# A cross-attention and mixture-of-experts layer on one core: another order of work at its beginning and in its last pair of batches

## The reference

```python
x = x + attention(layernorm(x), ctx)   # 16 heads of 16 channels, rotary positions on q and k,
                                       # query s sees keys s-64 .. s; projections q, k, v, o with biases
x2 = x
z = layernorm(x2)
top-2 of 8 experts by z @ router.T, softmax weights of the two
for each expert e:                     # gate, up: 1024x256, down: 256x1024
    y = (silu(z @ gate.T) * (z @ up.T)) @ down.T
    out += chosen(e) * y * mean weight of e over its tokens
```

## Time and profile before

| | before |
|---|---|
| median of 3 runs | 486.79 us (485.64 to 487.36) |
| profiled execution, own time | 483.92 us |
| its span | 482.1 us |
| TensorE (PE) busy | 446.3 us, 93% |
| VectorE (DVE) busy | 301.0 us, 62% |
| ScalarE (ACT) busy | 272.6 us, 57% |
| GpSimd (POOL) busy | 142.0 us, 29% |
| mean granted TensorE clock | 0.982 |

### The profile page before, as it was taken

How to read it: one execution, slowest core, us unless ns; L and a number is a source line. 1 busy time by engine, 2 the same in 40 slices (tenths; PEclk the granted TensorE clock), 3 DMA queues, 4 the chain that set the end, 5 groups by cost and what they waited for, 6 DMA issues and landing times.

```text
span 482.1 us, 8983 instructions
## 1 busy us (share of the span) xinstructions
PE 446.3 (93%) x2787; PEld 367.9 (76%) x2787; DVE 301.0 (62%) x735; ACT 272.6 (57%) x863; POOL 142.0 (29%) x174
## 2 busy tenths in 40 slices
PE   3898999999999999889999999999999999999980
PEld 2655666757565655569899999999999999999980
DVE  2565769898979878775737647466465473763330
ACT  1286887878788888335445545455464554554230
POOL 5111013544446262673023050140410502205013
PEclk9999999999999999989999999999999999999995
DMA  8173421111202020229956545565465553213002
GB/s 229 41 210 111 175 78 33 39 41 33 67 6 67 8 63 26 84 76 384 300 151 155 180 78 170 166 125 164 111 164 154 89 170 94 27 40 41 0 5 34
DMA packets 24588, 50.48 MB, mean 105 GB/s; under 512 B 5410, under 2 KB 15302, under 8 KB 24394
## 3 DMA queue, kind: packets, MB, share of 16 engines
q10 hardware_dynamic: 7886, 26.44, 17.6%
q1 hardware_dynamic: 10508, 16.47, 11.3%
q0 software_dynamic: 6144, 6.97, 8.8%
HBM read 39.62 MB, written 13.20 MB: 110 GB/s over the span
## 4 chain that ended last, share of the span: by engine, by line
PE 69%; DVE 7%; ACT 7%; DMA 5%; issue 5%; POOL 3%; ACTq 1%; POOLq 0%; SPq 0%; DVEq 0%
PE b_o L703 9%; PE b_small L703 8%; PE b_s L690 7%; PE b_s L692 7%; PE b_s L691 7%; PE b_s L445 6%; ACT probs L831 4%; PE b_pv L468 3%; PE b_proj L523 3%; PE b_pt L454 3%; PE b_pt L690 2%; PE b_pt L692 2%; PE b_pt L691 2%; PE b_proj L499 2%; DMA xin<-slots 2%
## 5 line engine op out<-in xcount | busy, mean ns | idle before, releaser
L831 ACT ACTIVATE probs<-b_s,negmax 100x100 f32<-100x100 f32 x256 | 85.4, 359 | 24.1 <-DVE negmax L1108 16.7
L1320 POOL DMA_INDIRECT out<-y_sb,idnow x32 | 49.7, 1552 | 158.7 <-ACT y_sb L869 151.4
L857 ACT CAST h_hi<-h_sb 128x448 fp32r<-128x448 f32 x64 | 36.3, 567 | 88.1 <-DVE h_sb L1185 88.1
L690 PE MATMUL b_s<-x_hi,w_hi 128*128 128x448 f32 x192 | 71.5, 372 | 0.0
L692 PE MATMUL b_s<-x_hi,w_lo 128*128 128x448 f32 x192 | 70.4, 367 | 0.0
L691 PE MATMUL b_s<-x_lo,w_hi 128*128 128x448 f32 x192 | 70.0, 364 | 0.0
L1086 DVE TENSOR_TENSOR w_lo<-w_raw,w_hi 128x1024 fp32r<-128x1024 f32 x48 | 58.8, 1225 | 13.8 <-ACT w_hi L792 13.4
L1189 DVE TENSOR_TENSOR h_lo<-h_sb,h_hi 128x448 fp32r<-128x448 f32 x64 | 40.0, 625 | 40.5 <-ACT h_hi L857 39.9
L831 ACT ACTIVATION_READ_ACCUMULATOR probs<-b_s,negmax 100x1 f32 x256 | 56.5, 221 | 0.0
L445 PE MATMUL b_s<-kblk,qrot 128*100 128x400 f32 x128 | 53.7, 500 | 0.0
L792 ACT CAST w_hi<-w_raw 128x1024 fp32r<-128x1024 f32 x48 | 50.4, 1050 | 0.0
(11 more groups left out here) (153 smaller groups left out, 969.5 us busy)
## 6 DMA issues: line engine op xcount, KB each, us to landing
w_raw<-in_ffw ACTq DMA_DIRECT2D x48, 512.0 KB, 3.9
xin<-slots SPq DMA_DIRECT2D x10, 449.8 KB, 4.4
slots<-in_padrows SPq DMA_DIRECT2D x9, 449.8 KB, 4.1
kblk<-krot SPq DMA_DIRECT2D x128, 12.5 KB
out<-x_all SPq DMA_DIRECT2D x8, 200.0 KB
ctx_all<-in_ctxT SPq DMA_DIRECT2D x1, 1200.0 KB, 6.5
x_all<-in_x SPq DMA_DIRECT2D x1, 1200.0 KB
attw<-in_wT ACTq DMA_DIRECT2D x2, 256.0 KB, 3.9
```

The lines of the kernel that those rows point to most:

```text
L690: pe.matmul(o, wh[:, c, cols], x_hi[:, c, :], start=(c == 0), stop=False)
L831: m = nc.scalar.activation(probs[:, N % 3, h, :], b_s[N % 3][0:S, h * S:(h + 1) * S], ACT.Exp, bias=negmax[:, N % 4, h:h + 1], accum_out=p ...
L857: nc.scalar.copy(h_hi[:, f, :], h_sb[:, f % 2, :]).then_inc(s_hhi, 1)
L1320: G.indirect_dma_start(out, bass.IndirectOffsetOnAxis(idnow[:, n:n + 1], 0), y_sb[:, n, :], None, bounds_check=TOK + TILE - 1, oob_is_err= ...
```

## The change

At the beginning:
- TensorE starts with 16 matmuls on a zeroed tile `blank` (`idle(16)`), and has more of them between the first projections.
- ScalarE loads its table with an Exp on `blank` right after its three loads; it also makes `ident_bf` and `mask_bf`. The query weights get a semaphore of their own (`s_wq`). The other loads move to SyncE, behind a wait for the constants `cst`.
- VectorE writes xn, rotates, and makes the eight key blocks of half c = 0 of pair 0 itself (`first_key_blocks`), by a multiplication with a 0/1 column for each head (`C_HEAD`). SyncE makes the other eight.

In the last pair:
- The rows that are transposed for the logits are only centred (`rows_center`); 1/deviation comes in at the difference of the two best logits.
- The sums over `chosen` and over the weights are made by TensorE with more matmuls in place of additions on VectorE and GpSimd.
- ScalarE makes three of the four comparisons, as `relu(1 - |slot - here|)` in two passes (`near_columns`); VectorE the fourth (`hot_column`). GpSimd makes the low parts (`rows_low`), and issues all eight last scatters behind its weight sums.
- `hidden` starts with the products that need the high part alone, and `take_ids(0)` stands behind block `FC - 3`.

```diff
@@ SyncE
             sp.dma_start(cst[:, :], consts).then_inc(s_cst, 16)
+            sp.wait_ge(s_cst, 16)
+            sp.dma_start(attw[:, 2:4], wT[:, 2:4]).then_inc(s_w, 16)
+            sp.dma_start(biasrow[:, :, :], brow).then_inc(s_w, 16)
+            sp.dma_start(rw_sb[:, :, :], rwT).then_inc(s_w, 16)
+            sp.dma_start(rows_sb[:, :], rownum).then_inc(s_w, 16)
             load_rows(1, 1, 2)
...
-                for c in range(DC):
+                for c in range(0 if i else 1, DC):
@@ TensorE
+            def idle(count):
+                for _ in range(count):
+                    pe.matmul(b_s[0][:, 0:QH * S], blank[:, 0:P], blank[:, :], start=True, stop=True)
...
                         warm(3)
+                        x2_transpose(NPAIR - 1)
...
+                if i == NPAIR - 1:
+                    pe.matmul(o[:, E:2 * E], ones_bf[0:S, 0:S], chosen[:, 0, :], start=False, stop=False)
+                    pe.matmul(o, ones_bf[0:S, 0:S], before[:, 0:1, :].to_broadcast([S, 2, E]),
+                              start=False, stop=True).then_inc(s_rk, 1)
...
-            pe.wait_ge(s_ch, NPAIR)
-            small_free()
-            pe.matmul(b_small[:, 0:E], ones_bf[0:S, :], before[:, 2, :],
-                      start=True, stop=True).then_inc(s_cnt, 1)
+            pe.wait_ge(s_rkc, NPAIR - 1)
+            for k, counts in enumerate((before[:, 0, :], chosen[:, 0, :], chosen[:, 1, :])):
+                m = pe.matmul(b_pt[:, 0:E], ones_bf[0:S, :], counts, start=(k == 0), stop=(k == 2))
+            m.then_inc(s_cnt, 1)
             warm(4)
             late_rows(NPAIR - 1)
...
+            for k in range(TOPK * 2 + 1):
+                part = wsel[:, k - 1, :] if k else wacc[:, :]
+                m = pe.matmul(b_o[:, 0:E], cst[0:S, C_ONE:C_ONE + P], part,
+                              start=(k == 0), stop=(k == TOPK * 2))
@@ ScalarE
+            def near_columns(i, b):
+                last = i == NPAIR - 1
+                a.wait_ge(s_here, 2 if last else 1)
...
+                nc.scalar.activation(onehot[:, b, :], slot_sb[:, :], ACT.Abs, bias=here[:, b:b + 1], scale=-1.0
+                                     ).then_inc(s_abs, 1)
+                a.wait_ge(s_abs, done)
+                nc.scalar.activation(onehot[:, b, :], onehot[:, b, :], ACT.Relu, bias=1.0, scale=-1.0
+                                     ).then_inc(s_hotA, 1)
@@ VectorE
+            def first_key_blocks(half):
+                v.wait_ge(s_krot, 1)
+                v.wait_ge(s_zero, 3)
+                for h in range(half * QH, (half + 1) * QH):
+                    V.tensor_scalar(kblk[:, 0, 0, h, :], krot[:, 0:2, :].rearrange("p b s -> p (b s)"),
+                                    cst[:, C_HEAD + h:C_HEAD + h + 1], None, ALU.mult).then_inc(s_kblk[0], 16)
...
+            def rows_center(i):
+                v.wait_ge(s_var2, i + 1)
+                for b in range(2):
+                    ins = V.tensor_scalar(xn[:, b, :], x_all[:, 2 * i + b, :], mv2[:, b, 0:1], None, ALU.subtract)
+                ins.then_inc(s_xc, 1)
...
-                    if e == 0 and split and f == FC - 5:
+                    if e == 0 and split and f == FC - 3:
                         take_ids(0)
@@ GpSimd
+                if i == NPAIR - 1:
+                    rows_low(NPAIR - 2)
                 if i == NPAIR:
-                    scatter(i - 2, range(TOPK))
-            scatter(NPAIR - 2, range(TOPK, TOPK * 2))
+                    rows_low(NPAIR - 1)
+            scatter(NPAIR - 2)
             scatter(NPAIR - 1)
```

More of the change, by code:

```diff
@@ L597, in late_rows @@
                 for b in range(2):
-                    pe.wait_ge(s_hot, 2 * (i - NPAIR + 2) + b + 1)
+                    if last and b == 0:
+                        pe.wait_ge(s_hot, 1)
+                    else:
+                        pe.wait_ge(s_hotA, 3 if last else b + 1)
                     for c in range(DC):
@@ L627, in _ @@
                         den_transpose(2 * i - 1)
-                    if n == 0 and i == NPAIR + 1:
-                        warm(3)
-                    if n == 0 and 0 <= i - 2 < NPAIR:
+                    if n == 0 and 0 <= i - 2 < NPAIR - 1:
                         x2_transpose(i - 2)
                     if n == 0 and i == NPAIR + 1:
-                        warm(2)
+                        warm(1)
                     if n == 3 and nxt:
+                        if i < 0:
+                            idle(2)
                         q_project(i + 1)
+                        if i < 0:
+                            idle(3)
                     if 0 <= N - 2 < NQ * NPAIR:
@@ L646, in _ @@
                     if n == 1 and nxt:
+                        if i < 0:
+                            idle(8)
                         xn_transpose(i + 1)
@@ L688, in hidden @@
                         if f == 0 and which == 0:
+                            pe.wait_ge(s_xhi, DC * t + c + 1)
+                        pe.matmul(o, wl[:, c, cols], x_hi[:, c, :], start=(c == 0), stop=False)
+                        pe.matmul(o, wh[:, c, cols], x_hi[:, c, :], start=False, stop=False)
+                        if f == 0 and which == 0:
                             pe.wait_ge(s_xlo, DC * t + c + 1)
-                        pe.matmul(o, wh[:, c, cols], x_hi[:, c, :], start=(c == 0), stop=False)
-                        pe.matmul(o, wh[:, c, cols], x_lo[:, c, :], start=False, stop=False)
-                        m = pe.matmul(o, wl[:, c, cols], x_hi[:, c, :], start=False, stop=(c == DC - 1))
+                        m = pe.matmul(o, wh[:, c, cols], x_lo[:, c, :], start=False, stop=(c == DC - 1))
                     m.then_inc(done, 1)
@@ L741, in _ @@
             a.dma_start(attb[:, :, :], bT).then_inc(s_wk, 16)
[L742 to L746, removed]
+            a.dma_start(attw[:, 0], wT[:, 0]).then_inc(s_wq, 16)
+            a.wait_ge(s_blank, 1)
+            nc.scalar.activation(table[:, :], blank[0:1, 0:1], ACT.Exp)
             def evac_proj(i, which, ready, done):
@@ L840, in _ @@
                         evac_proj(i + 1, 1, s_k, s_kc)
+                    if n == 0 and i < 0:
+                        a.wait_ge(s_cst, 16)
+                        nc.scalar.copy(ident_bf[:, :], cst[:, C_ID:C_ID + P]).then_inc(s_setup, 1)
+                        nc.scalar.copy(mask_bf[:, :, :], cst[:, C_MASK:C_MASK + S].unsqueeze(1)
+                                       .to_broadcast([P, QH, S])).then_inc(s_setup, 1)
                     if n == 2 and nxt:
                         evac_proj(i + 1, 0, s_q, s_qc)
+            near_columns(NPAIR - 1, 1)
             def x_high(t):
@@ L1142, in _ @@
                         destinations(i - 2)
[L1143 removed]
+                    if n == 5 and nxt and i >= 0:
                         q_rotate(i + 1)
```

165 lines of the change are left out of this document (113 added, 52 removed).

## The result

The changed kernel takes 490.48 us (median of 13 runs, 489.46 to 492.37), the kernel before 486.95 (13 runs, 484.73 to 489.95): ratio 1.0081, 95% interval 1.0059 to 1.0102, 3.5 us slower. The profiled execution has a span of 488.1, 6.0 more than that of before.

A forecast was written before the change was run, and what follows sets the result against it. TensorE, 93% busy, was taken as the bound, with time lost only where it stands or runs at half clock. Beginning -3.5, tile 1 +2.3 and clock +2.8 sum to +1.6 us: 488.4 on the median, range 485.5 to 491.5.

The forecast's parts named there:

- The beginning: Start of the kernel: VectorE's value write at 17.2 instead of 20.74, -3.5 us, handed through by attention.
- The last scatter unchanged: GpSimd, last pair: last scatter issued at 220.6, the time of before, with the beginning's 3.5 left out.
- The tile's start: TensorE begins the first expert tile at 213.7 instead of 214.98, with the beginning's 3.5 left out.
- rival 3: Clock falls in the last pair as before, delaying VectorE's count: 2 us more on tile 1, 490.5; chance 0.12.
- The copy directly behind the sixth block: VectorE's copy of tile 0's ids at 236.5, after 20.2 us of its own work, without waiting for the ids.
- Tile 1: TensorE goes on with tile 1 at 242.6 instead of 240.32, after the later ids copy: +2.3 us.
- The clock behind the gap: TensorE stands 6.5 us before tile 1, then runs at low clock: +2.8 us, bounds 0 and 3.4.
- the transposes waiting 5 us or more: Sign in the profile after: tile 1's transposes wait 5 us or more for a transfer; wrong if under 2.
- The chances: Probabilities against the kernel before: faster 0.30, within about 0.3% (1.5 us) 0.26, slower 0.44.
- (2): Last pair pays: tile starts early enough, tile 1 lands at 240 or before, no long gap: 482.5; chance 0.24.
- (1): Gap before tile 1 costs no clock, or the transfer lands fast; halves cancel: 485.6; chance 0.18.
- (4): Constants land last anyway, xn no earlier: the beginning gives -1 instead of -3.5, 491; chance 0.04.

The follow-up runs named there:

- e7: Kernel before with only the idle matmuls of the new beginning (16, 8, 2 and 3) added: 486.64 us, ratio 0.9999.
- e2: Kernel before with the copy of tile 0's ids moved behind the sixth hidden block: 493.06 us, ratio 1.0114.
- e12: Same program as e4 (kernel before with the new beginning alone), run again on another chip: 480.85 us, ratio 0.9909.
- e4: Kernel before with the change's beginning alone, old last pair: 479.67 us, ratio 0.9854.
- e9: Changed kernel, ids copy still behind the sixth block, with ten more matmuls of no use in the last pair: 486.23 us, ratio 0.9993.
- e1: Changed kernel with the copy of tile 0's ids put back behind the fourth hidden block: 482.83 us, ratio 0.9917.
- e3: Changed kernel with 28 matmuls of no use on TensorE ahead of tile 1's transposes: 488.70 us.
- e5: Kernel before with the change's last pair alone, ids copy left behind the fourth block: 488.07 us, ratio 1.0021.
- e8: e1 with ScalarE's three comparisons put back on VectorE: 482.36 us.
- e6: e1 with ten more matmuls of no use on TensorE in the last pair: 481.59 us, ratio 0.9892.
- e10: e9 with the copy of tile 0's ids behind the fifth hidden block instead of the sixth: 483.01 us.
- e11: e10 with the low parts on VectorE and two of pair 6's scatters ahead of GpSimd's last weight sums: 482.47 us, ratio 0.9926.

## Why the forecast came out as it did

The direction and the mechanism of the loss were right: the moved line, the wait it makes and the low clock behind it. The number, 488.4 against 490.48, is close partly by luck. It was made of two terms that were both too small, the gain of the beginning and the cost on the way to tile 1, and their errors have opposite signs.

- **The beginning, forecast -3.5.** The value write was 2.8 earlier in the profile of after, the 12th maximum 3.4; the low stretch at 46 us took part of it back, so that 2.1 were left at the last maximum. The value write alone is no measure of the gain (e7: as early, and nothing gained). On the medians the beginning alone is worth 5.5 to 7.5. The step that failed is the sum's base: it was made against one execution that lay 2.9 below the median, and the difference was left unexplained. Part of it is half clock: both projections of the old beginning run at it, until 21 us in the kernel before and until 26 in e2; the new one has it for 3.4 us or not at all (e12, e4). The prediction read the clock from the page as full there, although its own sum sets the projection's 1.59, called warm, where 3.03 stood.
- **The last scatter unchanged, forecast 220.6 in the time of before.** It came at 219.26, with the 2.1 added back 221.4; from the last maximum 27.9 against 27.1 before. ScalarE's and VectorE's savings did not reach GpSimd. Right to within 1.
- **The tile's start, forecast 213.7.** Measured 215.61, or 217.7 with the 2.1 added back: 4.0 late. The forecast had the last pair at full clock; it ran at 0.51 from 207 to 217. That is rival 3's mechanism, which I gave 0.12 because "four busy stretches close up". They did not: TensorE was busy 5.28 of 7 us before the fall, and then each placing matmul and each of the ten sums took about double. Ten more matmuls of no use took 4.2 out (e9). About 0.8 of the 4.0 was lost before the fall: ScalarE ended its four passes for pair 6 at 206.62 (208.7 with the 2.1 added back), forecast 207.9.
- **The copy directly behind the sixth block.** VectorE's count from the first product to the copy, forecast 20.2, was 20.1. Only its start was late.
- **Tile 1, forecast +2.3.** Measured 4.3 in absolute time, 6.4 from the last maximum, that is with the beginning taken out. e1 and e2 show that the moved line does it: 4.7 less one way, 6.3 more the other.
- **The clock behind the gap, forecast +2.8.** Measured 1.7 (e3: 1.8 on the medians, 1.7 in the profile).

In the profiles: -2.1 + 6.4 + 1.7 = +6.0, the difference of the spans, where the forecast had +1.6. On the medians it is +3.5: the profiled execution of the kernel before lies 3.0 below its median, that of the changed kernel 0.6 below. Some 1.8 of this stand at the beginning (3.5 between the means of the beginnings, 1.7 between these two profiles); the rest is not located.

Of the signs named, the copy without a wait, the transposes waiting 5 us or more and the low clock behind them came. The tile's start was to be 4.8 earlier and was 0.6 later; the last scatter was to be 3.5 earlier and was 1.3. The chances are added up wrongly: by the shares given there, faster is 0.34 and slower 0.40, not 0.30 and 0.44.

Of the rivals, (3) is in part what happened, beside the forecast and not in its place. (2), that the last pair pays, is refuted as built (e1 against e4: with the ids back the new last pair still lacks 2 to 3 us against the old one on the medians; e5 against before has 1, which is within its interval), and so are (1), by e3, and (4), by e4. What exactly lowers the clock in the new last pair more than in the old is open: not the comparisons' engine (e8); more matmuls in its waits remove it (e6, e9, e10).

## What to carry to other kernels

A step that takes in a transfer's result has a right place only for one pair of times: when the transfer lands, and when the engine gets there. Moving it later because the engine will be earlier is a bet on the engine; if that does not come true, the next transfer pays in full and the clock behind the gap on top. Where two changes are made together, time each alone: here one gave 5.5 to 7.5 us and the other hid it. A stretch with two chains of nearly the same length shows nothing when one alone is shortened (e7). And where one profiled execution differs from the median by more than the effect sought, find out in which stage before adding terms to it.

## What was unexpected of the hardware

- VectorE pays for small work beside GpSimd: `chosen`, 16 columns, took 1.04 beside GpSimd's subtraction of 512 columns (205.70 to 206.79) and ended 0.03 behind it. It takes 0.18 in the kernel before and 0.17 where the two do not meet (e8, e11). Here it was not on the chain, which ran over TensorE's placing matmuls. The first row is that of the changed kernel, the second one of e11:

```profile
205.78 1.04 DVE L1134 TENSOR_TENSOR chosen<-sel 100x16 bf16<-100x16 f32 x1
```

```profile
203.58 0.17 DVE L1135 TENSOR_TENSOR chosen<-sel 100x16 bf16<-100x16 f32 x1
```

- The same code has low stretches at different places from one execution to the next: at 46 us in five of the ten profiles with the new beginning. Their 16th maximum came at 60.2 to 61.1, that of the other five at 58.8 to 59.0.
- A granted clock of 1.00 at the start of a trace need not be the rate: hold it against the time of the matmuls there (3.03 for eight in the kernel before, 1.59 in the changed one).
